# Attention stage: broadcast copies read as single copies, writes and the inversion at other places in their queues, turned scores ahead of weighing and projections

## The reference

```
h = conv over pairs of tokens + mean of the pair, then LayerNorm (gamma, beta)   # (32, 188, 256)
h = h + attention(layernorm(h))          # 16 heads of 16; decay = exp(-0.01 |i-j|)
    q = x Wq;  latent = (x Wk + x Wv) Wdown;  k = latent Wup_k;  v = latent Wup_v
    scores = (q k^T / sqrt(256)) * decay;  out = softmax(scores) v  Wo
h = h + ffn(layernorm(h))                # 16 experts, each takes its top 752 of 6016 tokens, + a shared FFN
```

## Time and profile before

| | us |
|---|---|
| median of 3 runs (lowest, highest) | 2042.38 (2039.92, 2043.25) |
| profiled execution, its own time | 2044.36 |
| its span in the profile | 2042.2 |
| PE busy / DVE busy / ACT busy / POOL busy | 1732.3 / 1226.7 / 944.0 / 945.9 |
| TensorE's mean granted clock | 0.917 |

### The profile page before, as it was taken

The page is one execution under the profiler, slowest core; times in us unless marked ns, Lnnn a source line. Parts: engine busy times, 40 slices in busy tenths (PEclk is TensorE's granted clock), DMA queues, the critical chain, the costliest instruction groups (busy, mean ns, idle before and its releaser), DMA issues.

```text
span 2042.2 us, 47014 instructions
## 1 busy us (share of the span) xinstructions
PE 1732.3 (85%) x15406; PEld 1269.4 (62%) x15406; DVE 1226.7 (60%) x3822; ACT 944.0 (46%) x2157; POOL 945.9 (46%) x945
## 2 busy tenths in 40 slices
PE   6856677777777777776799995999999999999997
PEld 5854445555555555553577773777777777777775
DVE  3883566666666666665857775555555555555551
ACT  3534545455555455543533254444444444444442
POOL 3851233333333333323722232466666666666665
PEclk9985888888898888988899995999999999999999
DMA  5512433333343333332421114233433334444322
GB/s 176 185 61 70 100 96 94 92 99 95 95 103 96 95 94 98 94 92 60 122 47 31 31 28 155 81 95 96 107 104 101 107 93 114 98 97 98 95 31 29
DMA packets 172243, 186.70 MB, mean 91 GB/s; under 512 B 111480, under 2 KB 146808, under 8 KB 166008
## 3 DMA queue, kind: packets, MB, share of 16 engines
q1 hardware_dynamic: 145272, 141.18, 24.3%
q0 software_dynamic: 26880, 44.36, 10.8%
HBM read 134.59 MB, written 50.44 MB: 91 GB/s over the span
## 4 chain that ended last, share of the span: by engine, by line
PE 52%; issue 18%; DMA 15%; POOL 6%; DVE 4%; SPq 2%; ACT 2%; POOLq 0%; DVEq 0%; ACTq 0%
PE psum L1756 24%; PE psum L1773 12%; DMA weighed<-arena 10%; PE psum L1621 6%; PE psum L1641 4%; POOL arena L613 2%; DMA arena<-k_halves 2%; POOL hidden L591 1%; POOL arena L596 1%; SPq L475 1%; DMA arena<-arena 1%; PE psum L1736 1%; DMA inverse_sums<-arena 1%; POOL arena L631 1%; ACT arena L759 1%
## 5 line engine op out<-in xcount | busy, mean ns | idle before, releaser
L1756 PE MATMUL psum<-arena,hidden 128*128 128x376 f16 x3072 | 493.5, 323 | 1.2 <-DVE arena L1369 0.9
L658 POOL TENSOR_TENSOR arena<-arena 128x376 f16<-128x376 f32 x320 | 314.9, 986 | 357.3 <-ACT arena L759 355.9
L1756 PEld LDWEIGHTS psum<-arena,hidden 128*128 128x128 f16 x3072 | 301.0, 98 | 189.6 <-issue 1.8
L808 ACT ACTIVATE arena<-psum 128x376 f32<-128x376 f32 x384 | 184.4, 480 | 308.9 <-PE psum L1462 299.5
L759 ACT ACTIVATE arena<-arena 128x376 f16<-128x376 f32 (+5 forms) x610 | 283.7, 473 | 61.2 <-DVE arena L1305 44.9
L1133 DVE CUSTOM_DVE_ANT_0 arena<-psum,constants 128x188 f32<-128x188 f32 x768 | 236.8, 345 | 86.4 <-PE psum L1448 80.6
L613 POOL TENSOR_TENSOR arena<-arena 128x376 f16<-128x376 f32 x128 | 114.7, 900 | 369.7 <-ACT arena L759 366.6
L977 ACT ACTIVATE arena<-psum 128x376 f32<-128x376 f32 x256 | 123.7, 483 | 342.9 <-PE psum L1756 342.9
L1142 DVE TENSOR_TENSOR psum<-psum,constants 128x376 f32<-128x376 f32 x384 | 212.2, 553 | 112.0 <-PE psum L1474 111.4
L1773 PE MATMUL psum<-hidden,arena 128*128 128x256 f16 (+1 forms) x2304 | 256.6, 273 | 0.0
L759 ACT ACTIVATE arena<-psum 128x188 f32<-128x188 f32 (+7 forms) x457 | 176.2, 398 | 163.6 <-PE psum L1736 58.0
(11 more groups left out here) (158 smaller groups left out, 2747.7 us busy)
## 6 DMA issues: line engine op xcount, KB each, us to landing
arena<-e_g SPq DMA_DIRECT2D x16, 1024.0 KB
arena<-e_u SPq DMA_DIRECT2D x16, 1024.0 KB, 5.0
arena<-e_d SPq DMA_DIRECT2D x16, 1024.0 KB
arena<-x_t SPq DMA_DIRECT2D x32, 376.0 KB, 3.5
weighed<-arena POOLq DMA_DIRECT2D x32, 376.0 KB, 8.8
arena<-q_halves SPq DMA_DIRECT2D x192, 47.0 KB
arena<-k_halves SPq DMA_DIRECT2D x192, 47.0 KB
q_halves<-arena SPq DMA_DIRECT2D x32, 188.0 KB, 5.9
```

The costliest lines, as they stand in the source:

```text
L658: nc.gpsimd.tensor_tensor(dst, f, hi, ALU.subtract).then_inc(ready, 1)
L808: nc.scalar.activation(PT[:, i % 6 * 2 * S:(i % 6 + 1) * 2 * S], TB[i % 3], ACT.Exp).then_inc(exp_done, 1)
L1756: last = mm(bank[2 * (s % 2) + i][:, 0:CHUNK], w_, a, start=n == 0, stop=n == 5)
```

## The change

Four edits, all in the attention stage:

1. `read` without `blocks` issues three DMAs of 32 partitions each instead of one of 32 and one of 64 with a broadcast source. The bytes are the same. The two semaphore counts that PE awaits go from 8 to 9 DMAs for each batch.
2. SP's round: the write of the q halves goes ahead of the write of the inverse sums, and the write of the k halves ahead of the wait for the inverse sums' landing and of their four reads. POOL's round: the low half of k goes ahead of `dense_heads`.
3. DVE's `invert` goes from behind step 5 to behind step 8.
4. PE's step: `turned_scores` stands right behind `scores`, ahead of `weigh` and `job`.

```diff
@@ -463,11 +463,10 @@
             meet(sp)
 
             def read(blocks, dense, dram, c, single, par, landed):
-                both = 1 - single // 2
                 if blocks is None:
-                    for low, r, n in ((1, single, 1), (0, both, 2)):
-                        src = dram[c, low, :, :, :].rearrange("h (d a) n -> (h d) (a n)", a=HP)
-                        sp.dma_start(dense[par][32 * r:32 * (r + n), :], src.unsqueeze(0).broadcast_to((n, 32, HP * S)) if n > 1 else src).then_inc(landed[par], 16)
+                    for r in range(3):
+                        sp.dma_start(dense[par][32 * r:32 * r + 32, :],
+                                     dram[c, int(r == single), :, :, :].rearrange("h (d a) n -> (h d) (a n)", a=HP)).then_inc(landed[par], 16)
                 else:
                     for h2 in range(2):
                         for r in range(3):
@@ -499,6 +498,7 @@
                     hold(sp)
                     read(None, QX, q_dram, b + 1, 0, 1 - par, st_in)
                     read(KD, None, k_dram, b + 1, 2, 1 - par, st_in)
+                write(q_dram, b + 3, QS, ql_ready, q_out)
                 c = b - 1
                 if valid(c):
                     sp.wait_ge(sums_inverse, c + 1)
@@ -506,7 +506,7 @@
                     at_least(sp, rd_in, 64 * c)
                     hold(sp)
                     sp.dma_start(r_dram[:, :].rearrange("h (q n) -> (h q) n", q=4), RS[0:64, :]).then_inc(rs_out, 16)
-                write(q_dram, b + 3, QS, ql_ready, q_out)
+                write(k_dram, b + 3, KS2, kl_ready, k_out)
                 if valid(c):
                     sp.wait_ge(rs_out, 16 * c + 16)
                     hold(sp)
@@ -516,7 +516,6 @@
                     for g in range(4):
                         sp.dma_start(RD[64 * (g % 2):64 * (g % 2) + 64, g // 2 * S:(g // 2 + 1) * S],
                                      heads[g].unsqueeze(1).broadcast_to((4, HD, S))).then_inc(rd_in, 16)
-                write(k_dram, b + 3, KS2, kl_ready, k_out)
             batches(sp, spread_halves)
             meet(sp)
 
@@ -647,8 +646,8 @@
                 divide(b - 2)
                 low(OTL, ON, OTH, oth_ready, b - 2, otl_ready)
                 low(QS[:, 2 * S:4 * S], QF, QS[:, 0:2 * S], qh_ready, b + 3, ql_ready)
+                low(KS2[:, 2 * S:4 * S], KF, KS2[:, 0:2 * S], kh_ready, b + 3, kl_ready)
                 dense_heads(b - 1)
-                low(KS2[:, 2 * S:4 * S], KF, KS2[:, 0:2 * S], kh_ready, b + 3, kl_ready)
 
             batches(pool, batch)
             meet(pool)
@@ -1149,7 +1148,7 @@
                     times_decay(b, n)
                     if n == 0:
                         keep_moments(b - 3)
-                    elif n == 5:
+                    elif n == 8:
                         invert(b - 1)
                     elif n == 9:
                         low_max(b + 1, 1 - par)
@@ -1442,7 +1441,7 @@
                 c, cpar, i = ahead(b, par, n, LEAD)
                 if valid(c):
                     if i == 0:
-                        pe.wait_ge(s_in[cpar], 64 * c + 128 - 64 * cpar)
+                        pe.wait_ge(s_in[cpar], 72 * c + 144 - 72 * cpar)
                     at_least(pe, scaled, NS * c + i - 1)
                     for u, a, t in tiles_of(i):
                         last = mm(SB[i % 2][:, u * S:(u + 1) * S], block_tile(QD[cpar][0:2 * KR, :], a, t), KX[cpar][0:2 * KR, a * S:(a + 1) * S],
@@ -1468,7 +1467,7 @@
                 c, cpar, i = ahead(b, par, n, 1)
                 if valid(c):
                     if i == 0:
-                        pe.wait_ge(st_in[cpar], 64 * c + 128 - 64 * cpar)
+                        pe.wait_ge(st_in[cpar], 72 * c + 144 - 72 * cpar)
                     at_least(pe, exp_done, NS * c + i - 2)
                     for u, a, t in tiles_of(i):
                         last = mm(TB[i % 3][:, u * S:(u + 1) * S], block_tile(KD[cpar][0:2 * KR, :], a, t),
@@ -1592,12 +1591,12 @@
                 for n in range(NS):
                     take_max(b, par, n)
                     scores(b, par, n)
+                    turned_scores(b, par, n)
                     if n == 1:
                         weigh(b - 1, 1 - par, 3)
                     elif n % 3 == 1:
                         weigh(b, par, (n - 4) // 3)
                     job(b, par, n)
-                    turned_scores(b, par, n)
 
             batches(pe, batch)
             meet(pe)
```

## The result

The changed kernel takes 1886.32 us (median of 4 runs, 1886.1 to 1888.54) against 2042.82 us of the kernel before in the same job: ratio 0.9236, 95% interval 0.922 to 0.9252. Forecast were 1918 us, in a range of 1870 to 1980. The profiled execution has a span of 1883.9 us, 158.3 less than before, where 126 were forecast.

A forecast was written before the change was run, and what follows sets the result against it. Waits, chiefly PE's for KX, late from a copy on two DMA engines, were taken as the bound. Saving 28 x (24.3 - 20.2) = 115 us, plus 8 in first and 3 in last rounds, gave 1918 us, range 1870 to 1980.

The forecast's parts named there:

- The round: 20.2 forecast: Full attention round, set by SP's list: 16.7 us of issues and gaps plus the inverse sums' landing, against 24.3 now.
- The three dense issues: SP's list: issuing the three copies takes 1.73 us for KX and again for QX.
- the chain through step 6: From KX's landing through step 6, the inverse sums and next KX issues to its landing: 19.7 us, just below SP's list.
- L: Landing time of the inverse sums' write in SP's round: 3.5 us taken, bounds 1.7 and 5.8.
- The stages' ends: Attention stage outside full rounds: some 8 us saved in the first rounds, 3 in the last.
- forecast +0.2 us a round: SP's list: q write ahead of the inverse sums costs 0.85 us, k write inside their wait saves 0.63.
- DVE's 3.4 us: DVE's wait a round before the reciprocal, for the sums; inverting behind step 8 was to remove it without a new stall.
- The bounds of -2.0 and +3: Turned scores ahead of jobs: us of compute a round, put at 0 in full rounds because SP's list hides it.
- The compute-bound one: Rival: PE sets full rounds at 17.1 to 18.4 us, total near 1875 us; chance 0.17.
- The slower one: Rival: landings unimproved, inversion at step 8 delays the chain to 26.8 us a round, total 2112 us; chance 0.05.
- 12.7 + L + l: Round length of the chain through step 6, with l the landing of KX: 3.5 us taken, bounds 3.2 and 8.3.
- The partly better rival: Rival: small pieces keep landings slow, both chains 21.7 to 23.7 us a round, total 1965 to 1995 us; chance 0.17.

The follow-up runs named there:

- e1: Kernel before with only the dense reads split into three 32-row copies: 1850.24 us, ratio 0.9049.
- e2: Changed kernel with the broadcast copy back, keeping the moved writes, inversion and turned scores: 2037.08 us, ratio 0.996.
- e10: e1 with halves tensors padded so each 32-row copy's DRAM source has a slowest dimension of 2: 2112.73 us, ratio 1.0349.
- e3: Changed kernel with `turned_scores` back at the end of PE's step: 1887.07 us.
- e4: Changed kernel with DVE's reciprocal back behind step 5: 1881.2 us, ratio 0.9204.
- e5: Changed kernel with the q and k writes and POOL's order as before: 1847.98 us.
- e6: e1 with only the q write moved ahead of the write of the inverse sums: 1877.49 us.
- e7: e1 with the k write moved inside the wait for the inverse sums, with POOL's order for it: 1845.73 us.
- e11: e7 with `turned_scores` right behind `scores`: 1834.71 us.
- e9: e8 with `turned_scores` right behind `scores`: 1810.68 us, ratio 0.8867.
- e8: e1 with the four reads of the inverse sums moved from SP's to POOL's queue: 1841.94 us.

## Why the prediction was right, and where it was off

**The cause was right.** That two DMA engines hold up KX, and by their backlog all later DMAs, was read from a share of 0.14 while everything waited. e1 shows that splitting the copy alone brings the whole gain and more, e2 that without it there is none, and e10 that neither the broadcast nor the copy's size is needed for the loss, only a slowest dimension of 2.

**The round: 20.2 forecast, 19.5 measured.** SP's list does set it. Take SP's waits off the round and the same remains in every kernel that has edit 1 and leaves the reads of the inverse sums to SP: 16.9 to 17.1 us in after, e1, e3, e4, e5, e6, e7 and e11. It was 18.2 before. The kernels differ by the waits alone, 0.7 to 2.5 us a round. Three terms of the forecast were mis-sized. The three dense issues take 1.4 us on average and not 1.73, since I priced each like half of a pair in which one was the two-engine copy: 0.7 us a round too much for both reads. KX lands 1.9 us after its last issue in the round above, 2.1 in the median of the 28, not 3.5, so the chain through step 6 never came near. From the start of the inverse sums' write to the four reads it is 3.9 us on average (4.5 in the round above), not the 3.5 of L: 0.4 us too little. All the rest of the list is 15.7 us and not 16.7.

**The stages' ends: 11 us forecast, 24 measured.** The first rounds brought 14.3 us, not 8: I counted the k landings on the chain and not the q writes behind the same engines, whose longest piece on the chain ahead of the first inverse-sum write went from 7.4 to 4.1 us. The row of before:

```profile
187.54 7.39 DMA q_halves<-arena
```

The last rounds brought 9.8 and not 3; e1, without edit 4, already has 6.1 of them (1131.9 us behind the 29th write before, 1125.8 in e1), so transfers carry most of these as well.

**Edit 2: forecast +0.2 us a round, measured +1.4.** I gave L one value, 3.5, and asked only what the order costs in SP's list. For the order as changed that value was no luck: the prediction gave the q write alone 2.4 us (e6 has 2.5) and named POOL's reads of `weighed` as coming on top, and after has 3.6. The step that failed most is that L got no value of its own for the order as it was: it is 1.7 us in e5. The order around the write isn't all, though: e1, e9 and e11 have the inverse sums ahead of both writes as well, and L there is 2.4, 2.8 and 2.6. What differs is POOL. The full rounds of the ten kernels with edit 1 and whole 32-row copies, by what was issued just ahead of the inverse sums' write (mean landing, rounds):

| | no read of `weighed` in the 2.5 us ahead | a read of `weighed` within 1.5 us ahead |
|---|---|---|
| q write not ahead (e1, e5, e7, e8, e9, e11) | 1.8 (75) | 2.8 (74) |
| q write ahead (after, e3, e4, e6) | 2.5 (24) | 3.7 (67) |

The other 40 rounds, with a read 1.5 to 2.5 us ahead, lie between. So the q write just ahead goes with 0.7 to 0.9 us more, and POOL's reads with 1.0 to 1.2. In after they fall together; in the round above the second read went out 0.17 us ahead of the write, which took 4.4 us to land:

```profile
489.95 0.60 POOL L630 DMA_DIRECT2D arena<-weighed  x1
```

In after, e3 and e4 the k write also stands 0.7 us behind the inverse sums. The two effects come to 3.5 us without it (2.5 and 1.0), and the only round of e6 with a read just ahead took 3.5, so little is left for it. All this is read from rounds as they fell: no run moved POOL's reads alone, or the k write alone at that distance.

**Edit 3: the move did not remove DVE's 3.4 us.** The forecast gave them to the move. e1 and e4 have the reciprocal behind step 5 and wait 0.1 and 1.0 us in 28 rounds: the sums land earlier with the transfers mended, and the move brings nothing, or costs the 5 us by which e4 is faster.

**Edit 4: hidden, as forecast, and worth 31 us uncovered.** e3 shows 0.8 us of difference under SP's list. With SP out of the way (e8 to e9) it takes 0.95 us off a round. The bounds of -2.0 and +3 held; the cost that I feared, PE waiting for an exponential, is not among the waits of e9 that matter: the weight loads of its `turned_scores` stood 5.9 us in 28 rounds.

**The rivals.** The compute-bound one fell for this kernel; its estimate of 17.1 us lies between the 17.9 and 16.9 of e8 and e9, where compute sets the round. The slower one has its place right (e2's SP does wait 4.1 us a round for the reciprocal) and its price wrong: I added the largest L and the largest landing of KX as if both could hold at once, yet in e2 the later write landed in 2.9 us. 12.7 + L + l with that L and its round of 24.3 leaves l at 8.7, near the 8.3 of before.

**Sums of the prediction that don't come out.** By its own 1918 at 20.2 us, rounds of 19.5 to 21.3 us give 1898 to 1949, not 1888 to 1940; with L at 1.7 it gives 1868, just under the range that was to hold it. The partly better rival has a chain of 23.7 us, which leaves 28 x 0.6 = 17 us and not 45. The compute-bound rival's 17.1 us would give 28 x 7.2 + 11 = 213 us, down to 1829 and not 1855. The forecast of 1918 doesn't rest on these. Of the 32 us between it and the measured 1886.3, 19 come from the round and 13 from the stage's ends.

## What to carry to other kernels

When the engines wait and the DMA share stands at a small fraction, read it as a number of DMA engines: here 0.12 to 0.14 was two of 16, and it led to the copy whose slowest dimension was 2. Copies of 32 rows cured it, even at the price of one DMA more for each read. A small DMA that lands slowly can be a symptom of the same backlog, so don't move it about before that is gone: here the orders that were changed along with the cure took 36 us of its gain back. Once it is gone, look at what is issued just ahead of a small DMA that others wait for, on every queue: here the q write and POOL's reads made 3.7 us out of 1.8. Sum the issuing queue's list without its waits; where it is nearly the round, its waits are what is left to win. And judge an order of compute in a kernel where nothing else binds; the same move was worth nothing under SP's list and 31 us without it.

## What the runs showed of the hardware that was not expected

SP's issue time differs with the shape of the copy: three dense reads took 1.38 us with 32 rows as the slowest dimension and 2.2 with a slowest dimension of 2 (e10), 0.46 against 0.73 us each, for the same bytes and count. Whether the number of DMA engines or the one dimension more in e10's source costs this time, no run tells apart. The row of e10:

```profile
619.29 2.19 SPq L468 DMA_DIRECT2D arena<-k_halves  x3
```

PE's granted clock fell to 0.50, the 1.2 GHz level, for some 3 us after it had stood 2.07 us in after; one of these microseconds:

```profile
507.00:508.00 1.00, 1.00 (x16) 0.20 (x8) 1.00 (x6) 0.34 (x1) 0.58 (x1) 0.50 0.43 90
```

Over the full rounds the mean clock is 0.94 there. It is 0.96 in e4 with 2.0 us a round of waiting for KX, 0.97 in e3 with 1.4, 0.99 in e5 and e6 with 1.3, and 1.00 in e1 with 0.4. Less waiting thus paid twice, as forecast from the earlier trace rows.
